# A vision mixer on one core: most of the output stage is moved, in slices, into the scan of the next image

## The reference

```python
def _mamba(x_seq, W_in, conv_w, conv_b, W_xproj, W_dt, b_dt, A_log, D, W_out):
    xz = x_seq @ W_in
    x, z = (xz[..., :D_INNER], xz[..., D_INNER:])
    x = _silu(_causal_conv(x, conv_w, conv_b))
    proj = x @ W_xproj
    dt = jax.nn.softplus(proj[..., :DT_RANK] @ W_dt + b_dt)
    Bm = proj[..., DT_RANK:DT_RANK + D_STATE]
    Cm = proj[..., DT_RANK + D_STATE:]
    A = -jnp.exp(A_log)
    y = _selective_scan(x, dt, Bm, Cm, A, D)
    return y * _silu(z) @ W_out
...
out_fwd = _mamba(x_seq, *mparams)
out_bwd = jnp.flip(_mamba(jnp.flip(x_seq, 1), *mparams), 1)
out = out_fwd + out_bwd
```

## Time and profile before

| | |
|---|---|
| time, median of 3 runs | 6108.0 us (6099.7 to 6111.59) |
| profiled execution: time, span | 6094.89 us, 6093.1 us |
| convolution, pointwise, normalise, weights | 0 to about 868 us |
| scan | about 868 to 5825 us |
| output | 5825.5 to 6093.1 us |
| DVE busy | 5283.2 us (87%) |
| POOL busy | 5086.4 us (83%) |
| PE busy | 4619.8 us (76%) |
| ACT busy | 3208.8 us (53%) |
| mean granted TensorE clock | 0.728 |

### The profile page before, as it was taken

The page is one execution under the profiler, slowest core; times in us unless marked ns, Lnnn a source line. Parts: engine busy times, 40 slices in busy tenths (PEclk is TensorE's granted clock), DMA queues, the critical chain, the costliest instruction groups (busy, mean ns, idle before and its releaser), DMA issues. The chain is left out here.

```text
span 6093.1 us, 73704 instructions
## 1 busy us (share of the span) xinstructions
PE 4619.8 (76%) x17228; PEld 1200.3 (20%) x17228; DVE 5283.2 (87%) x3520; ACT 3208.8 (53%) x5155; POOL 5086.4 (83%) x2403
## 2 busy tenths in 40 slices
PE   7999737777777777777777777777777777777779
PEld 6776211111111111111111111111111111111123
DVE  3224729999999999999999999999999999999943
ACT  1225635555555555555555555555555555555533
POOL 0000429999999999999999999999999999999966
PEclk9999866666666766667666666766666766666789
DMA  1002845555555555555555555555555555555599
GB/s 34 28 28 81 224 123 182 182 182 183 183 181 181 184 182 180 182 179 184 184 182 181 180 180 183 183 182 182 183 182 184 183 182 180 180 180 179 184 268 278
DMA packets 351021, 1048.26 MB, mean 172 GB/s; under 512 B 66820, under 2 KB 101430, under 8 KB 300556
## 3 DMA queue, kind: packets, MB, share of 16 engines
q1 hardware_dynamic: 334976, 1022.36, 53.2%
q10 hardware_dynamic: 16012, 25.53, 1.3%
HBM read 836.01 MB, written 211.63 MB: 172 GB/s over the span
## 5 line engine op out<-in xcount | busy, mean ns | idle before, releaser
L1267 POOL TENSOR_TENSOR hc<-hring,c_rep 128x1024 f32<-128x1024 f32 x1539 | 3591.2, 2358 | 104.5 <-DVE hring L1230 90.7
L1230 DVE TENSOR_TENSOR_SCAN hring<-decay,carry,u_ps 128x1024 f32<-128x1024 f32 x1219 | 2815.9, 2331 | 0.0
L1212 DVE TENSOR_TENSOR u_ps<-u_ps,u_rep 128x1024 f32<-128x1024 f32 x1220 | 1474.4, 1209 | 152.9 <-PE u_ps L1035 152.8
L1125 ACT ACTIVATE decay<-dt_rep,w_a 128x1024 f32<-128x1024 f32 x1221 | 1395.1, 1146 | 309.4 <-DVE hring L1230 308.0
L1053 PE MATMUL y_ps<-hc,w_gather 128*32 128x512 f32 x6144 | 1191.5, 860 | 460.8 <-POOL hc L1267 453.3
L1035 PE MATMUL u_ps<-stack_b,w_spread 48*128 48x512 bf16 x2440 | 1021.0, 508 | 623.7 <-DVE hring L1230 620.1
L1125 ACT ACTIVATE u_ps<-dt_rep,w_a 128x1024 f32<-128x1024 f32 x321 | 358.9, 1118 | 1033.7 <-DVE hring L1230 1033.7
L1254 POOL TENSOR_TENSOR drive_p<-u_rep,b_rep 128x1024 f32<-128x1024 f32 x322 | 760.9, 2363 | 26.9 <-DMA u_rep<-u_scr 26.9
L1230 DVE TENSOR_TENSOR_SCAN hring<-u_ps,carry,drive_p 128x1024 f32<-128x1024 f32 x321 | 750.5, 2338 | 0.0
L582 POOL TENSOR_TENSOR xs<-xc_ln,rs 96x512 f32<-96x512 f32 x64 | 90.2, 1410 | 683.0 <-ACT rs L566 673.5
L1077 PE MATMUL prep_ps<-xn,w_conv 128*128 128x512 f32 x792 | 558.1, 826 | 71.5 <-DMA xn<-xn_scr 69.9
(11 more groups left out here) (108 smaller groups left out, 3927.7 us busy)
## 6 DMA issues: line engine op xcount, KB each, us to landing
dt_rep<-dt_scr SPq DMA_DIRECT2D x194, 1024.0 KB, 5.8
u_rep<-u_scr SPq DMA_DIRECT2D x194, 1024.0 KB, 7.5
c_rep<-bc_scr SPq DMA_DIRECT2D x260, 512.0 KB, 4.0
b_rep<-bc_scr SPq DMA_DIRECT2D x130, 512.0 KB, 6.4
xn<-xn_scr SPq DMA_DIRECT2D x132, 384.0 KB, 6.5
y_scr<-y_sb SPq DMA_DIRECT2D x768, 64.0 KB, 3.2
xn<-xn_scr SPq DMA_DIRECT2D x132, 256.0 KB, 6.7
dt_scr<-dt_sb SPq DMA_DIRECT2D x260, 128.0 KB, 2.1
```

The costliest lines, as they stand in the source:

```text
L1125: nc.scalar.activation(to[:, :], dt_rep[r][:, b, :], ACT.Exp, scale=w["a"][:, col:col + 1]).then_inc(decay_ready, 1)
L1212: nc.vector.tensor_tensor(slot[:, :], slot[:, :], u_rep[r][:, b, :], ALU.mult).then_inc(drive_ready, 1)
L1230: nc.vector.tensor_tensor_scan(hring[nv % NHR][:, ::step], factor[:, ::step], term[:, ::step], carry[:, drv, nv:nv + 1], ALU.mult, ALU.add ...
L1267: nc.gpsimd.tensor_tensor(hc[nv % NHC][:, :], hring[nv % NHR][:, :], c_rep[q][:, :], ALU.mult).then_inc(c_applied, 1)
```

## The change

1. Of the eight images, the first seven get their output inside `scan`: in each pass, from the eighth on, one slice of 512 tokens of the image before is treated (57 slices loaded, 56 stored). `output` keeps the last image alone: 8 slices in place of 64.
2. The slice work is laid out as 128 partitions x 768 elements instead of 96 x 1024. SP loads it with seven DMAs at step 15 and stores it with one at step 12. TensorE makes z at steps 21 and 23 and projects at step 10, all through `prep_ps`. ScalarE copies z out, takes its Silu beside the preparation's, and copies the result. VectorE does the sum (`SUM_Y_AT`) after its front of step 1 and the product (`GATE_AT`) after that of step 4. The sum was GpSimd's before.
3. ScalarE takes each result from `prep_ps` one step after TensorE made it, and the steps of the tables are moved: CONV_AT now puts two of the three matmuls of a group in one step; DT_AT is 4, 6, 8.
4. LEAD is 8 instead of 6, so that the gather, and all of prep and conv, come two units later against the scan; `hc` has 8 buffers for it.
5. u is written over `soft` instead of into a buffer of its own; ScalarE waits for its store.

```diff
-LEAD = 6
+LEAD = 8
...
-        NDA, NSLOT, NHR, NHC = 4, 3, 4, 6
+        NDA, NSLOT, NHR, NHC = 4, 3, 4, 8
...
         SILU_AT = 0
         LOW_AT = 2
-        DT_AT = (4, 5, 6)
-        CONV_AT = ((8, 9, 10), (12, 13, 14), (16, 17, 18))
-        SUM_AT = (6, 11)
-        U_AT = (8, 13)
-        BSPLIT_AT = 10
-        XN_AT = 2
-        BC_AT, B_RAW_AT, B_SPLIT_STORE_AT, STACK_AT = 4, 7, 12, 15
-        B_AT = (13, 12)
-        C_AT = (16, 18, 20, 22)
-        DT_STORE_AT = (7, 13)
-        U_STORE_AT = (9, 15)
+        DT_AT = (4, 6, 8)
+        CONV_AT = ((12, 12, 13), (15, 15, 16), (18, 18, 19))
+        SUM_AT = (7, 9)
+        U_AT = (8, 10)
+        BSPLIT_AT = 5
+        XN_AT = 0
+        BC_AT, B_RAW_AT, B_SPLIT_STORE_AT, STACK_AT = 4, 5, 7, 8
+        B_AT = (11, 7)
+        C_AT = (14, 16, 18, 20)
+        DT_STORE_AT = (10, 12)
+        U_STORE_AT = (11, 13)
...
+        SLICE_AT, Z_AT = 15, (21, 23)
+        SUM_Y_AT, GATE_AT, PROJECT_AT, RES_AT, OUT_STORE_AT = 1, 4, 10, 11, 12
+        SLICE_DMAS = 7
...
+            with eng.Fori(0, CHUNKS - 1) as it:
+                iteration(it, (False, False), (False, False))
+            iteration(CHUNKS - 1, (False, True), (False, False))
+            with eng.Fori(CHUNKS, ITERS) as it:
+                iteration(it, (True, True), (True, True))
...
# SP
+                        wait(sp, z_made, made, k)
+                        wait(sp, projected, free, k)
+                        sp.wait_ge(y_stored, stored)
+                        sp.dma_start(xz[:, :], d["xn_scr"][image, :, bass.ds(at + HALO, SL)]).then_inc(slice_in, 16)
+                        for to, scr in ((y_fwd, d["y_scr"][0]), (y_bwd, d["y_scr"][1])):
+                            sp.dma_start(to[:, 0:SL], scr[image, 0:P, bass.ds(at, SL)]).then_inc(slice_in, 16)
+                            for s in range(2):
+                                sp.dma_start(to[64 * s:64 * s + 64, SL:], scr[image, P:DI, bass.ds(at + s * (SL // 2), SL // 2)]).then_inc(slice_in, 16)
...
# TensorE
+                    if m == Z_AT[0]:
+                        pe.wait_ge(slice_in, 16 * SLICE_DMAS * (k + 1))
+                        pe.wait_ge(prep_out, NPREP * (k + OUT_LAG + 1) + 3)
+                        nc.tensor.matmul(prep_ps[:, :], w["z"][:, 0:P], xz[:, :], start=True, stop=True).then_inc(z_made, 1)
...
+                    if m == PROJECT_AT:
+                        pe.wait_ge(gated, k + 1)
+                        pe.wait_ge(prep_out, NPREP * (k + OUT_LAG + 2))
+                        for s in range(2):
+                            cols = slice(s * (SL // 2), (s + 1) * (SL // 2))
+                            nc.tensor.matmul(prep_ps[0:C, cols], w["out"][:, 0, :], y_bwd[:, cols], start=True, stop=False)
+                            mm = nc.tensor.matmul(prep_ps[0:C, cols], w["out"][:, 1 + s, :], y_bwd[:, SL:], start=False, stop=True)
+                        mm.then_inc(projected, 1)
...
# ScalarE
+                        if slicing:
+                            act.wait_ge(z_out, 2 * (pn - OUT_LAG))
+                            nc.scalar.activation(z_sb[:, :], z_sb[:, :], ACT.Silu).then_inc(z_silu, 1)
...
-                    if m in DT_AT:
-                        g = DT_AT.index(m)
+                    if m - 1 in DT_AT:
+                        g = DT_AT.index(m - 1)
...
# VectorE
+                    if m == SUM_Y_AT:
+                        dve.wait_ge(slice_in, 16 * SLICE_DMAS * (k + 1))
+                        nc.vector.tensor_tensor(y_fwd[:, :], y_fwd[:, :], y_bwd[:, :], ALU.add).then_inc(y_sum, 1)
+                    if m == GATE_AT:
+                        dve.wait_ge(y_sum, k + 1)
+                        dve.wait_ge(z_silu, k + 1)
+                        nc.vector.tensor_tensor(y_bwd[:, :], y_fwd[:, :], z_sb[:, :], ALU.mult).then_inc(gated, 1)
...
# GpSimd
-                            nc.gpsimd.tensor_tensor(u_sb[:, HALVES[h]], dt_sb[:, HALVES[h]], xa[dr][:, HALVES[h]], ALU.mult).then_inc(u_ready, 1)
+                            nc.gpsimd.tensor_tensor(soft[:, HALVES[h]], dt_sb[:, HALVES[h]], xa[dr][:, HALVES[h]], ALU.mult).then_inc(u_ready, 1)
```

More of the change, by code:

```diff
@@ L88, in over_slices, with over_last @@
     image(B - 1, last=True)
+def over_last(eng, *stages):
+    most = max(lead for lead, _ in stages)
+    for s in range(-most, NS):
+        for lead, what in stages:
+            if 0 <= s + lead < NS:
+                what(s + lead)
 def after(eng, sem, count):
@@ L634, in weights @@
             loads.append((wx[rows, col, :], d["w_x"][lo:hi, h, :]))
+            loads.append((out_w[rows, col, :], d["w_out"][lo:hi, h, :]))
             for k, name in enumerate(("conv_b", "dt_b", "skip")):
@@ L846, in run, with iteration @@
                         what(n, n, 0, 0)
-            with eng.Fori(0, ITERS) as it:
+            def iteration(it, gates, slices):
                 for dr in range(2):
@@ L858, in run @@
                             elif kind == "prep":
-                                what(m, p + 1, it + dr, 1 - dr)
-                            else:
-                                what(m, p + 2, it + 1, dr)
+                                what(m, p + 1, it + dr, 1 - dr, slices[dr])
+                            elif kind == "conv":
+                                what(m, p + 2, it + 1, dr, slices[dr])
+                            elif kind == "gate" and gates[dr]:
+                                what(m, p + 1 - OUT_LAG, it + dr, 1 - dr)
+                            elif kind == "slice" and slices[dr]:
+                                what(m, p - OUT_LAG, it, dr)
                     for kind, what in tasks:
@@ L1188, in back, with gate, slice_out @@
                     nc.scalar.copy(y_sb[:, :], y_ps[:, :]).then_inc(y_ready, 1)
+                def gate(m, k, it, dr):
+                    if m == Z_AT[0] + 1:
+                        wait(act, gated, k, k)
+                        act.wait_ge(z_made, 2 * k + 1)
+                        nc.scalar.copy(z_sb[:, 0:SL], prep_ps[:, :]).then_inc(z_out, 1)
+                    if m == Z_AT[1]:
+                        act.wait_ge(z_made, 2 * k + 2)
+                        nc.scalar.copy(z_sb[:, SL:], prep_ps[:, 0:SL // 2]).then_inc(z_out, 1)
+                def slice_out(m, k, it, dr):
+                    if m == RES_AT:
+                        act.wait_ge(projected, k + 1)
+                        wait(act, out_stored, 16 * k, k)
+                        nc.scalar.copy(res[:, :], prep_ps[0:C, :]).then_inc(res_ready, 1)
                 act.wait_ge(zeroed, 1)
                 load_exp_ln(nc)
-                run(act, ("back", back), ("front", front), ("prep", prep), ("conv", conv))
+                run(act, ("back", back), ("front", front), ("prep", prep), ("slice", slice_out), ("conv", conv), ("gate", gate))
             @block.vector
```

177 lines of the change are left out of this document (111 added, 66 removed).

## The result

The changed kernel takes 6220.5 us (median of 4, 6219.2 to 6223.3), that of before 6107.2 in the same comparison: a ratio of 1.019, interval 1.018 to 1.0205. It is 1.9% slower. The forecast was 6082, faster by 26. The time lies inside the wide range (5995 to 6230), outside that of the likeliest case (6035 to 6120), and the sign is wrong.

The account below looks back on a forecast made before the run. The scan was taken to be bound by VectorE's own work, with TensorE's lateness on top. 56 x (1.7 + 0.6 + 1.0) = 185, plus 4 and 8, less 223, gave -26 us: 6082, likeliest 6035 to 6120, wide 5995 to 6230.

Parts of the forecast that it names:

- the likeliest case: The forecast itself: 6082 us, a pass with a slice growing by 3.3 us; chance 0.43, own range 6035 to 6120.
- VectorE's two operations: Sum and product in the scan, 56 times: 1.7 us a pass of own time plus 0.6 waiting for GpSimd's running operation.
- The product's 0.2: Product's wait in the scan: hc of 9 ends 0.1 to 0.2 us after S(10), the end of the scan of 10.
- The sum's 0.4: Sum's wait: hc of 6 ends 0.4 us after S(7), S(v) being the end of the scan of v.
- GpSimd goes ahead at the port: Rival, chance 0.06: GpSimd's queued operation precedes waiting VectorE; 8.4 us a pass instead of 0.6, 6519; sign, operations of 3 us and more.
- Own time, 1.7: VectorE's sum and product in the scan: 0.85 us each, 1.7 a pass, with no cover.
- Stalls, 2.2 against 1.16: VectorE's stalls a pass in the scan: 0.9 + 0.9 + 0.2 + 0.2 = 2.2 us against 1.16, so 1.0 more.
- all low: Stalls a pass in the low case: 0.9 + 3.0 + 2.5 + 0.2 = 6.6 us, so 5.4 more.
- the late Ln: GpSimd after the scan of 12: done at 3.5 us, waits for ScalarE's Ln until 4.6; scans of 18 to 20 lose 1.1.
- The distance of the gather: LEAD 8 in the scan: losing TensorE's wait for hc before the gather is worth at most 1.16 us a pass.
- The output stage, 44 us: Output after the scan: with eight slices the stage ends at 5869.7, about 44 us long, saving 223 us.
- stalls don't grow: Rival, chance 0.16: gather distance frees TensorE, port waits are short; a pass grows 1.7 to 2.3 us, 6010 in all.

Follow-up runs that it names:

- sum_step3: Changed kernel with VectorE's sum moved from step 1 to step 3 (after the scan of unit 9); 5983.3 us, ratio to before 0.979.
- no_sum: Changed kernel without VectorE's sum in the slices, its waits kept (seven images' output lacks the backward scan); 5937.2 us, ratio to before 0.973.
- lead6: Changed kernel with LEAD 6 instead of 8, sum at step 5 and product at step 6, behind the scans of 9 and 10; 6142.3 us, ratio to before 1.007.
- run_broken: Changed kernel with one more GpSimd wait: before hc 5, until its own hc 4 is done; 5984.5 us, ratio to before 0.979.
- port_probe5: Changed kernel plus a stage of 24 rounds with further already met waits ahead of GpSimd's products; after 13 products VectorE's sum still ended 0.81 us after the one met.
- port_probe2: Changed kernel plus a fifteen-round stage: four GpSimd products in a row, VectorE's sum arriving at varied points of the second; it ended 0.81 us after that product.
- sum_gpsimd: Changed kernel with the sum on GpSimd, after its hc of 8 (step 3), instead of on VectorE; 6299.5 us, ratio to before 1.031.
- port_probe4: Changed kernel plus an 18-round stage varying GpSimd's row length, product size and a wait for its own result; 13 products let VectorE's sum in, 14 did not.
- gate6_alone: Changed kernel without the sum and with the product moved from step 4 to step 6, after the scan of 12; 5922.8 us.

## Why the prediction was wrong

**The step that failed** is the one on VectorE's two operations: "It waits for GpSimd's running operation to end, then runs", which made 0.6 us a pass. Measured: the sum waits 5.20 - 0.93 = 4.27, the product 1.10 - 0.93 = 0.16 us, 4.4 together. The product's 0.2 was right. The sum's 0.4 missed two things. With hc 7 ready behind hc 6 it isn't the next border that counts: 2.3 us. And the placement was off too: "Shortly before unit 7 GpSimd has caught up: hc of 5 starts at S(5)" was put down without a row, and hc 5 starts 1.7 us after S(5) on the mean of the passes with a slice, so that hc 6 ends 2.0 us after S(7) instead of 0.4 (1.5 in the stretch shown above): 1.6 us. In all 56 x (4.4 - 0.6) = 213 us: the forecast of 6082 with that is 6295. Of the 75 us between that and 6220 the stalls (below) are 64; another 11 are that the two profiled executions differ by 124, the medians by 113.

The rival *GpSimd goes ahead at the port* had the mechanism, at 0.06, and priced it wrong, at 8.4 us a pass (6519 in all): it applied one rule to both operations. Its sign, an operation of 3 us and more, came for the sum alone. The sum lost (4.27 measured, 2.73 in the rival), the product did not (0.16, not 5.7). The sentence "No row shows a back-to-back GpSimd against a waiting VectorE" was true, and it was a reason to give the unknown more weight. The rows that I argued from the earlier trace rows show GpSimd with gaps around each add, the case in which VectorE goes at the border.

The wait is for whole instructions: every operation that had to wait ends 0.8 to 0.9 us (a whole sum) behind the end of some GpSimd instruction. Being issued first did not decide it: the sum was issued at 3033.13, hc 7 began at 3034.6, and hc 7 went first. Who goes next was worth 237 us here.

**Own time, 1.7.** Right: 0.85 for each of the two in the trace of sum_step3, 0.82 for a sum by no_sum.

**Stalls, 2.2 against 1.16.** Wrong, and it hid part of the miss. Measured in the changed kernel: (122.5 - 77.2) / 64 = 0.7 us a pass for spreads, 10.5 / 64 = 0.2 for the ring, 0.1 for decays: 1.0, so 0.15 less where 1.0 more was forecast, 56 x 1.15 = 64 us. In it the sum's long wait gives TensorE 4 us of time, but sum_step3, without that, shows 1.0 as well (0.45 for spreads, 0.57 for ring and decays). Of the two spreads that TensorE's clumped matmuls were to make 0.9 us late each, one came: up to 0.93 and 0.66 on the mean before the drive of 18, nothing before that of 20. No run shows TensorE's terms in the forecast's sum of stalls (0.9, 0.9 and the first 0.2, and 3.0 and 2.5 for "all low"). The changed kernel shows in their place a projection of 3.73 us (median of 56, at a granted clock of 0.52 on the mean) and behind it a gather of 1.07 and a skip of 1.04 us (medians); each of these takes 1.93 where the clock is 0.50, but it is at 1.00 again 4.3 us after the projection's start on the mean. The ScalarE side of it came too: GpSimd waits (94.9 us over 65 times) about 1.5 us for the late Ln, 1.1 by the forecast's times (3.5 to 4.6).

**The distance of the gather** was given no more than the 1.16 us of today's stalls. In lead6 it is 3.28 - 0.45 = 2.8 us a pass in spreads, of which 159 / 63 = 2.5 reach the time. But 2.2 of these are there in the passes without a slice, so they are no sign of the slices' load; they belong to the tables of the changed kernel run with LEAD 6. How much the distance by itself was worth stays open.

**The output stage, 44 us.** Measured: 6217.4 - 6172.74 = 44.7. The loads of the slices and z's Silu never held VectorE (no idle time before either operation), as forecast.

**The rival "stalls don't grow"** gave 6010 for the changed kernel. Once the sum finds the port its case is there: the growth is 78.5 - 76.7 = 1.8 us a pass (1.7 to 2.3 by the rival), and sum_step3 is 5983, run_broken 5984. The change itself is worth 2.1%, and its step for the sum turned that into a loss of 1.9%.

**Left open.** That the row's length decides is shown by putting gaps in it and by the stages; why it does is not. Nor is why the turn is at 14 of GpSimd's products in the stage, between 6 and 12 instructions in the scan, and one or two later with half-size products: waits between them don't do it (port_probe5), and other differences (VectorE's scans, transfers, register instructions beside the row) weren't tried.

## What to carry to other kernels

When an instruction with two SBUF operands is put on VectorE beside a nearly full GpSimd, price it by the length of GpSimd's unbroken row, not only by the instruction that is running: here it cost the rest of that instruction behind a short row, and everything that stood ready behind a long one. How long is long has to be measured in the kernel at hand (here it was 14 in the stage and fewer in the scan). Put it where GpSimd has just run dry, or let GpSimd wait for its own last result a few instructions ahead: 0.1 us there was worth 236 us here. And where no row shows who wins, look for a row in the same condition (back to back, not just overlapping) before a rival is put at 6 in 100.

## What the runs showed of the hardware

- In the added stages (port_probe2 to port_probe5) a VectorE sum of two SBUF tiles that meets a 128x1024 product of GpSimd ends 0.81 us after the end of that product after up to 13 products in an unbroken row, and from 14 on only when GpSimd has nothing ready (7.7 us after it with three queued, 12.3 with five). A gap made by a wait of GpSimd for its own result let VectorE in at 0.07 us (sum_gpsimd) and at 0.14 us (port_probe4), and one of under 0.03 us, from a wait for VectorE's scan, did in no_sum.
- The wait stands in the trace as busy time of VectorE (5.2 us for 0.93 us of work in the changed kernel), without any idle time or releaser; the sign of it is a duration that is too long for the shape and an end 0.8 us behind an end of GpSimd's.
- VectorE holding the port lengthens GpSimd's instruction in turn: in the changed kernel the drive behind the product took 3.06 us (3.055 to 3.08 in the 56 passes with a slice), where the median of all such drives is 2.37.
- A float32 matmul leaves two records in the changed kernel's trace (L1132, the gather: 6144 for two matmuls in each of 64 x 24 units), a bfloat16 one leaves one (L1114, the spread: 2442 for 1221 drives of two each). A record of the convolution's first two groups, 512 columns, takes 1.06 us where the granted clock is 0.50 of full speed and 0.59 us where it is 1.00 (medians).
- The product of gate6_alone takes 2.12 us instead of the 1.11 of no_sum, and the kernel is no slower (5922.8, timed once, against 5937.2). VectorE's waits for spreads fell from (117.9 - 79.3) / 64 = 0.6 us a pass to (80.7 - 78.7) / 64 = 0.03, those before the scans from 0.3 to 0.1: 0.8 of the 1.0 us back. The rest, and the 14 us, are not explained. A wait for the port can stand in the place of a wait that would come anyway.
